# First gates and values moved into the front, the last step reordered, and decay rows carried by 9 transfers per sequence in place of 24

## The reference

```python
alpha = jax.nn.sigmoid((x @ Wg + bg) / GATE_NORM)          # one gate per token and head
def step(state, inp):
    qt, kt, vt, at = inp
    state = at[..., None, None] * state + kt[..., None] * vt[:, :, None, :]
    out_t = jnp.einsum('bhk,bhkv->bhv', qt, state)
    return (state, out_t)
...
return out * og @ Wo

gates = jax.nn.softmax(x @ Rw, axis=-1)                     # 3 experts, per token
base = x @ W + b
zg = (x @ A) * gates                                        # LoRA, rank 8 per expert
return base + SCALING * (zg @ Bm)
```

## Time and profile before

| | us |
|---|---|
| median of three runs | 528.37 |
| lowest and highest | 527.98 and 529.04 |
| profiled execution, its own time | 528.53 |
| its span, first to last instruction | 526.4 |
| TensorE busy in the span | 490.9 (93%) |
| VectorE and ScalarE busy | 352.1 (67%) and 341.9 (65%) |
| granted TensorE clock, mean | 0.966 |

### The profile page before, as it was taken

How to read it: one execution, slowest core, us unless ns; L and a number is a source line. 1 busy time by engine, 2 the same in 40 slices (tenths; PEclk the granted TensorE clock), 3 DMA queues, 4 the chain that set the end, 5 groups by cost and what they waited for, 6 DMA issues and landing times.

```text
span 526.4 us, 11885 instructions
## 1 busy us (share of the span) xinstructions
PE 490.9 (93%) x4560; PEld 392.3 (75%) x4560; DVE 352.1 (67%) x1012; ACT 341.9 (65%) x647; POOL 170.0 (32%) x241
## 2 busy tenths in 40 slices
PE   8689989998999999998899999999999887999995
PEld 6557867786778778876578787787777676888884
DVE  6887887787777977462587677775778562544533
ACT  3968967795768688955467676676666534565541
POOL 3510550035003102200435727447274441443311
PEclk8879999999999999998899999999999997999998
DMA  8600000000001200000342241231312000001001
GB/s 304 186 1 2 2 0 1 0 2 1 0 1 42 98 1 1 2 0 27 94 116 73 60 112 46 77 90 52 100 46 76 2 3 0 22 21 40 21 21 41
DMA packets 24251, 23.44 MB, mean 45 GB/s; under 512 B 3809, under 2 KB 22945, under 8 KB 24065
## 3 DMA queue, kind: packets, MB, share of 16 engines
q1 hardware_dynamic: 23136, 22.12, 13.8%
q10 hardware_dynamic: 1056, 0.52, 0.4%
HBM read 20.27 MB, written 2.36 MB: 43 GB/s over the span
## 4 chain that ended last, share of the span: by engine, by line
PE 43%; ACT 4%; DVE 2%; issue 2%; POOL 2%; DMA 1%; SPq 1%; DVEq 0%; POOLq 0%; ACTq 0%
PE bank L2044 6%; PE bank L1958 5%; PE bank L168 5%; PE bank L170 5%; PE bank L169 5%; PE bank L1983 3%; PE bank L2009 3%; PE bank L1998 3%; PE bank L1971 2%; PE bank L2036 2%; PE bank L244 2%; ACT att_qT L1773 1%; PE bank L2052 1%; ACT lora_zT L1769 1%; DVE att_prob L1420 1%
## 5 line engine op out<-in xcount | busy, mean ns | idle before, releaser
L1069 PE MATMUL bank<-ffn_g_hi,w_hi 128*128 128x512 f32 x288 | 116.8, 406 | 0.1
L1070 PE MATMUL bank<-ffn_g_lo,w_hi 128*128 128x512 f32 x288 | 114.1, 396 | 0.0
L610 DVE TENSOR_TENSOR ffn_g_lo<-ffn_full,ffn_g_hi 128x512 fp32r<-128x512 f32 x96 | 67.1, 699 | 27.4 <-ACT ffn_full L856 26.0
L1069 PEld LDWEIGHTS bank<-ffn_g_hi,w_hi 128*128 128x128 f32 x288 | 54.3, 189 | 13.9 <-issue 1.7
L1070 PEld LDWEIGHTS bank<-ffn_g_lo,w_hi 128*128 128x128 f32 x288 | 54.3, 189 | 11.7
L856 ACT ACTIVATE ffn_full<-bank,cols 128x512 f32<-128x512 f32 x64 | 44.3, 697 | 20.9 <-PE bank L1070 14.7
L1608 POOL TENSOR_TENSOR att_vw<-att_v,att_prob 128x128 f32<-128x128 f32 x64 | 25.2, 421 | 88.1 <-DVE att_prob L1420 88.1
L1800 ACT COPY att_qT<-bank 128x512 f32<-128x512 f32 x64 | 37.1, 589 | 12.8 <-PE bank L170 8.6
L1420 DVE TENSOR_TENSOR_SCAN att_prob<-att_prob,bank 128x512 f32<-128x512 f32 x32 | 37.4, 1204 | 7.7 <-DMA att_prob<-cut_rows 7.6
L1431 DVE TENSOR_TENSOR att_prob<-bank,att_prob 128x512 f32<-128x512 f32 x32 | 21.9, 691 | 29.8 <-PE bank L1958 27.8
L712 POOL TENSOR_TENSOR ssm_out_rstd<-ssm_out_var,neg_half 128x4 f32<-128x4 f32 x8 | 9.2, 1154 | 82.3 <-DVE ssm_out_var L491 82.3
(11 more groups left out here) (230 smaller groups left out, 1181.8 us busy)
## 6 DMA issues: line engine op xcount, KB each, us to landing
att_prob<-cut_rows SPq DMA_DIRECT2D x64, 128.0 KB, 3.0
att_wide<-cum_rows SPq DMA_DIRECT2D x64, 56.0 KB
out<-att_vw SPq DMA_DIRECT2D x7, 256.0 KB, 2.3
x<-in_x SPq DMA_DIRECT2D x3, 512.0 KB, 11.8
w_raw<-in_w_all SPq DMA_DIRECT2D x1, 1152.0 KB
w_raw<-in_w_all SPq DMA_DIRECT2D x1, 768.0 KB, 9.6
x<-in_x ACTq DMA_DIRECT2D x2, 256.0 KB, 3.5
w_raw<-in_w_all SPq DMA_DIRECT2D x1, 512.0 KB, 4.8
```

The costliest lines, as they stand in the source:

```text
L610: dve.tensor_tensor(lo, full[j % 4][:, :], hi.bitcast(F32), ALU.subtract).then_inc(low, 1)
L1069: pe.matmul(acc, w[0], x[0], start=start, stop=False)
L1070: return pe.matmul(acc, w[0], x[1], start=False, stop=stop)
```

## The change

Three things are edited. **One:** the gates and values matmuls of sequence 0 stand in the front, the gates behind tile 21 of the last pair, the values at its very end, and ScalarE's gates and the save of `cut` there too. VectorE then runs all four scans of sequence 0 ahead of its first `weigh`. **Two:** in step 7 the router of sequence 0 and 1, the exponentials, `join`, `low_h`, `down(1)` and `flip_in(9)` have other places. **Three:** the DRAM copies of `cut` and `cum` have another layout, and a sequence takes 9 transfers in place of 24.

```diff
-        r["cut_rows"] = nc.dram_tensor("cut_rows", (B, NH, 2, Q), F32, kind="Internal").ap()
-        r["cum_rows"] = nc.dram_tensor("cum_rows", (B, NH, S), F32, kind="Internal").ap()
+        r["cut_rows"] = nc.dram_tensor("cut_rows", (B, 2, GLO, Q), F32, kind="Internal").ap()
+        r["cum_rows"] = nc.dram_tensor("cum_rows", (B, GLO, S), F32, kind="Internal").ap()
...
+def save_cut(sp, r, b, saved):
+    for u in range(2):
+        rows = r["cut_rows"][b, u].rearrange("g (t n) -> t g n", n=C)
+        sp.dma_start(rows, r["cut"][b % 2][:, u * C:(u + 1) * C]).then_inc(saved, 16)
...
-                    for t in range(T):
-                        sp.dma_start(r["cut_rows"][b, :, :, t * C:(t + 1) * C], by_chunk(cut[b % 2][gate_rows(t), :])).then_inc(cut_saved, 16)
...
-                    for t in range(T):
-                        sp.dma_start(r["cum_rows"][b, :, t * P:(t + 1) * P], cum[b % 2][gate_rows(t), :]).then_inc(cum_saved, 16)
+                    sp.dma_start(r["cum_rows"][b].rearrange("g (t n) -> t g n", n=P), cum[b % 2][:, :]).then_inc(cum_saved, 16)
...
                     for q in range(2):
-                        for u in range(2):
-                            heads = r["cut_rows"][b, g * PER + 2 * q:g * PER + 2 * q + 2, u, :]
-                            sp.dma_start(prob[n % KEEP][half_rows(u), 2 * q:2 * q + 2, :], over(heads, 0, [C, 2, Q])).then_inc(spread_in[n % KEEP][q], 16)
+                        first = g * PER + 2 * q
+                        heads = r["cut_rows"][b, :, first:first + 2, :].rearrange("u h n -> u (h n)")
+                        dst = prob[n % KEEP][:, 2 * q:2 * q + 2, :].rearrange("p h n -> p (h n)")
+                        sp.dma_start(dst, over(heads, 1, [2, C, S])).then_inc(spread_in[n % KEEP][q], 16)
...
-                    for k in range(NH):
-                        rows = slice(k % PER * DV, (k % PER + 1) * DV)
-                        sp.dma_start(wide[b % 2][rows, k // PER, C:S], r["cum_rows"][b, k:k + 1, C:S].broadcast_to([DV, S - C])).then_inc(wide_ready, 16)
+                    for q in range(2):
+                        heads = r["cum_rows"][b, q * PER:(q + 1) * PER, C:S]
+                        dst = wide[b % 2][:, q, C:S]
+                        sp.dma_start(dst, over(heads, 1, [PER, DV, S - C])).then_inc(wide_ready[b % 2], 16)
...
+                                if j == 21:
+                                    gate_mm(pe, claim(pe, "alpha", 0), r, r["h_full"][0]).then_inc(mm, 1)
...
+                    for k in range(2):
+                        value_mm(pe, claim(pe, "ahead", k), r, [x[:, :] for x in h[0]], k).then_inc(r["ahead"], 1)
...
-                alpha(0)
-                values(0)
                 for k in range(AHEAD):
                     query(0, k)
...
-                for j in range(LEAD):
+                for j in range(PAIRS):
                     scan(0, j)
...
+                    if not n:
+                        route(0, 0)
                     weigh(b, 2)
                     weigh(b, 3)
-                    if not n:
-                        route(0, 0)
...
+                across(LAST, 0)
+                route(1, 0)
+                across(LAST, 1)
                 moments(B + 2)
-                route(1, 0)
...
-                    join(b)
+                        join(b)
+                low_h(B + 1)
+                join(LAST)
+                rescale(B + 2)
                 gate(LAST)
-                low_h(B + 1)
-                rescale(B + 2)
```

More of the change, by code:

```diff
@@ L94, in build @@
         r["wg"] = sb("wg", [P, GLO])
+        r["cut"], r["start"] = [sb(f"cut{n}", [P, P]) for n in range(2)], sb("start", [P, P])
+        r["ahead"], r["cut_saved"] = ctx.enter_context(nc.semaphore("ahead")), ctx.enter_context(nc.semaphore("first_cut_saved"))
         r["ones"] = sb("ones", [P, P])
@@ L396, in loop_uses @@
                         uses.append((("spread", j - 9), 6 + j - 15))
+                    if i == 3 and j == 21:
+                        uses.append((("alpha", 0), 6))
                 uses.append((("y", 2 * i), 4))
             uses += [(("y", B - 1), 5), (("yflip", B - 2), 4), (("yflip", B - 1), 5)]
+            uses += [(("ahead", 0), 0), (("ahead", 1), 1)]
             return uses
@@ L763, in _ @@
                     pool.wait_ge(att_h_ready, b + 1)
-                    pool.tensor_tensor(h[b][1][:, :], r["h_full"][b][:, :], h[b][0][:, :].bitcast(F32), ALU.subtract)
+                    pool.tensor_tensor(h[b][1][:, :], r["h_full"][b][:, :], h[b][0][:, :].bitcast(F32), ALU.subtract).then_inc(att_h_low, 1)
+                for tile in (*r["cut"], r["start"]):
+                    pool.memset(tile[:, :], 0.0).then_inc(blank, 1)
             @block.scalar
@@ L955, in _ @@
                     bring_y(2 * i)
+                act.wait_ge(blank, SLOTS + 1)
+                act.wait_ge(bias_kept, 1)
+                act.wait_ge(mm, full_at("alpha", 0))
+                cut_gates(act, r, r["cut"][0], bank("alpha", 0))[0].then_inc(cut_ready, 1)
                 bring_y(B - 1)
@@ L1212, in attention_lora @@
         og = pair("og", [P, 2, S])
-        cut, cum = pair("cut", [P, P]), pair("cum", [P, P])
-        start = sb("att_start", [P, P])
+        cum = pair("cum", [P, P])
         ends, total = pair("ends", [P, NC, NH]), pair("total", [P, NC, NH])
@@ L1335, in __init__ @@
             def __init__(self):
-                self.made = 0
+                self.made = GIVEN
             def __call__(self, pe, *use):
@@ L1549, in _ @@
                     weigh(b, 1)
-                    scan(b, 2)
-                    scan(b, 3)
+                    if b:
+                        scan(b, 2)
+                        scan(b, 3)
                     if n:
@@ L1794, in values @@
                     for k in range(2):
-                        act.wait_ge(ring_mm, full("v", b, k))
+                        if b:
+                            act.wait_ge(ring_mm, full("v", b, k))
+                        else:
+                            act.wait_ge(r["ahead"], k + 1)
                         act.copy(v[s][:, 2 * k:2 * k + 2, :].rearrange("p c n -> p (c n)"), bank("v", b, k)[:, :]).then_inc(v_ready, 1)
@@ L1843, in _ @@
                 keep_htok(0)
-                for b in range(B):
-                    n = b + 1 < B
-                    if n:
-                        gates(b + 1)
+                for b in range(LAST):
+                    gates(b + 1)
                     for k in range(AHEAD, NH):
@@ L1850, in _ @@
                     out_gates(b)
-                    if n:
-                        values(b + 1)
+                    values(b + 1)
                     keep_states(b)
                     keep_inner(b, 0)
-                    if not n:
-                        exps(0, 0)
                     normalise(b + 2)
-                    if n:
-                        for k in range(AHEAD):
-                            query(b + 1, k)
-                    else:
-                        ranks(0, 0)
-                        for m in range(KH):
-                            relu(0, m)
+                    for k in range(AHEAD):
+                        query(b + 1, k)
                     keep_inner(b, 1)
-                    if n:
-                        keep_total(b + 1)
+                    keep_total(b + 1)
                     bring_h(b + 2)
-                    if n:
-                        keep_htok(b + 1)
+                    keep_htok(b + 1)
+                for k in range(AHEAD, NH):
+                    query(LAST, k)
+                out_gates(LAST)
+                act.activation(table[:, :], r["neg_half"][:, :], ACT.Exp)
+                exps(0, 0)
+                keep_states(LAST)
+                keep_inner(LAST, 0)
+                normalise(B + 1)
+                ranks(0, 0)
+                for m in range(KH):
+                    relu(0, m)
+                    if m == 1:
+                        bring_full(B + 1)
+                    if m == 2:
+                        bring_high(B + 1)
+                keep_inner(LAST, 1)
                 exps(1, 0)
+                ranks(1, 0)
                 normalise(B + 2)
-                ranks(1, 0)
                 for b in range(1, B):
@@ L1914, in alpha @@
                     ps = claim(pe, "alpha", b, 0)
[L1915 to L1917 removed]
+                    gate_mm(pe, ps, r, hT[b % 2]).then_inc(ring_mm, 1)
                 def values(b):
@@ L2082, in _ @@
                             query(b + 1, k)
-                    else:
-                        flip_ranks(0, 0)
-                        for m in range(KH):
-                            layer1(0, m)
-                    inside(b, 1)
-                    cross(b, 0)
-                    if n:
+                        inside(b, 1)
+                        cross(b, 0)
                         totals(b + 1)
-                    flip_in(b + 2)
-                    if n:
+                        flip_in(b + 2)
```

(10 more changed lines are left out.)

112 lines of the change are left out of this document (60 added, 52 removed).

## The result

The changed kernel takes 620.29 us, median of 4 executions (619.29 to 621.16), beside 528.17 for the kernel before (526.04 to 529.04): the ratio is 1.175, with an interval of 1.171 to 1.179. It is 92 us slower. The forecast was 613 (592 to 655), with the mechanism of two DMA engines.

What follows compares the result with a forecast made beforehand. Two DMA engines per spread were taken to bound the kernel: sequence 0's data at 265.1, sequence 1's 304.3, six periods of 31.7 to 494.5, `states` 496.7, plus 117.8 - 5.4 + 1.6, plus 2.1 outside: 613 us, range 592 to 655.

Steps and rivals of the forecast that it cites:

- Two engines per spread: Engines divide both sides' outermost sizes; a spread reading [2, C, S] into 128 partitions gets 2. Forecast's chance 0.77.
- The rival of sixteen engines: Chance 0.13: split by SBUF or write side, spreads run on 16 engines, steps stay 21.4 us, end 516.3.
- Time of one spread: 131,072 B on each of two engines at 24.5 GB/s: 5.35 us, within 5.06 and 6.4; four make 21.4.
- The front: Start of sequence 0: front ends about 240.6, block starts 241.9, first spread packets move at 243.3 us.
- The period: Time per sequence in later steps: busiest engine 28.1 us plus 3.6 for turn-rounds, 31.7; six of them.
- turn-rounds: Empty queue between a save's last packets and the next spread's first: 1.8 us, twice per sequence, 3.6.
- First interval, last data to last data: From sequence 0's last scan data to sequence 1's, with both att_wide sets between: 8.2 + 2 x 4.8 + 21.4 = 39.2 us.
- The tail: From sequence 7's `states` to the end: 117.8 us, less 5.4 (2 to 7) for step 7's new order, plus 1.6.
- the lower clock: TensorE enters `states` of sequence 7 after long idling and runs at half clock: 1.6 us lost.
- `normalise` waiting for `join` and `rescale`: In step 7's new order, `normalise`, and `flip_in` with it, wait for these: some 1.9 us lost.
- The rival of instruction loads stuck behind full engines: Chance 0.06: TensorE's code loads wait behind 5.35 us transfers, 20 us per step, half hidden: 683 us.
- It decides from some 5 engines on: Engine count separating the cases: at 4 a sequence takes 21.0 us, even with the step.

Runs made afterwards that it cites:

- all on 16: Changed kernel with each spread cut into two halves and att_wide sent by single heads, so both use 16 engines; saves left: 513.47 us, ratio 0.969.

## Why the forecast came out, step by step

**Two engines per spread: right, and shown.** Cutting the transfers so that 16 engines take part gives back 107 us, and 4 engines in place of 2 give 66 (620.3 to 554.1). The rival of sixteen engines, at 516.3, describes the repaired kernel (513.5). The rule of the Trainium skill that I had cited holds in all of these; its row in the section "Rules for kernel authors" on using all 16 engines (DMA: Bandwidth & Descriptors) even names a short outermost dimension as the trap. Another row of that table would have led into it: it calls two transfers to the two halves of the partitions a waste and asks for one over 128. Here the measurement decides against that row as it stands, because in this layout the one transfer has the two halves outermost.

**Time of one spread: 5.35 forecast, 5.12 measured,** 25.6 GB/s per engine, at the fast bound of the earlier trace rows. The last data of sequence 0 were forecast for 265.1 and came at 264.50.

**The front: 241.9 forecast for the block's start, 240.95 measured.** In the other executions with this front SyncE issues the first spread between 240.93 and 242.47, so the forecast lies inside the scatter. With two engines per spread the front is worth 2.9 us at `states` of sequence 7. Where they don't bind, it brings 4.9 to 7.8 us in three profiles; the rival of sixteen engines had 6.8.

**The period: 31.7 forecast, 32.99 measured.** This is the term that was too small. My 28.1 + 3.6 against the measured parts:

- Spreads, four times 5.12 = 20.5, where I had 21.4. `att_wide` 4.8 forecast, and 4.83 by the run without it.
- What is left is 33.0 - 20.5 - 4.8 = 7.7, and I had 1.9 for the saves and 3.6 for the two turn-rounds, 5.5. So the halves of the loop have 2.2 us more in them than I took from the earlier trace rows, where a save went by an empty queue. The GB/s of the changed kernel between 341.2 and 354 us have a piece in them in which one of two engines seems to be idle:

```profile
GB/s 45 51 51 51 51 51 51 51 51 64 93 82 30 26 38 26 26 26 26 26 51 51 51 51 51 102 51 51 51 51 51 51 51 51 51 51 38 42 22 0
```

The eight slices at 26 to 38 (0.32 us each) are the rate of one engine; they follow the save of `cum`, and a like piece of 2.4 us stands in the other half of the period. At a turn-round the engines move nothing for 1.5 us, as the slices of 0.1 us from 339 to 343 show, and as long around 354 and 373:

```profile
GB/s 33 38 36 36 28 3 0 0 0 0 0 0 0 0 0 0 0 0 0 0 0 20 41 20 41 82 41 41 41 82 41 41 41 82 41 41 41 82 41 41
```

By my estimate from these slices the 7.7 us are 3.0 for two turn-rounds (I had 3.6), 2.5 lost to the two pieces at half rate (I had nothing), and 2.2 for the saves (I had 1.9). So the term that I had left out is the half rate. Why one engine would stop there was not tried, and stays open.

**First interval, last data to last data: 39.2 forecast, 41.6 measured** (264.50 to 306.09). Less 20.5 for the spreads and 9.7 for two sets of `att_wide`, 11.4 are left for three saves and three turn-rounds, and I had 8.2 for them: 1.1 too little for each, as in the period.

**The tail: too small a term, in the other direction.** I had 5.4 for the new order, within 2 and 7, less 1.6 for the lower clock. The changed kernel has 617.3 - 507.23 = 110.1 us from `states` of sequence 7 to the end, where before had 117.8: 7.7, not 3.8. Three things make up the 3.9, to 0.1.

- The low stretch of the clock over `layer1` of sequence 0, 1.7 us, which I hadn't priced, is in the kernel before alone. The new order by itself is worth 6.0 to 6.5: 116.1 with the old one against 110.1 and 109.6 (513.3 - 403.7) with the new one.
- I had charged 1.9 us for `normalise` waiting for `join` and `rescale`. The only gap of TensorE near there in the changed kernel is this, 0.7 less:

```profile
531.88 0.66 PE L246 MATMUL bank<-cols,norm_out 128*128 128x128 f32 x4 [1.20 <-ACT norm_out L1801]
```

- The lower clock, for which I had charged 1.6, came as forecast but cost nothing. In the changed kernel TensorE works through the 8.27 us behind the start of `states` at 0.83 without a gap. In the kernel with the new order alone it has the full clock there and waits 0.78 and 0.76 us for ScalarE; both take 110.1 us to the end.

```profile
507.23:515.50 8.27, 8.27 (x116) 6.51 (x115) 5.04 (x16) 4.12 (x11) 5.00 (x13) 0.83 0.01 2
```

Before, waits of 1.43 and 2.67 stood near the gap of 1.20, and 5 us at a clock of 0.51 behind them. Now the clock keeps its upper level, 2.4 GHz, as I had reckoned:

```profile
526.00:539.00 13.00, 11.37 (x76) 9.60 (x75) 4.74 (x29) 6.51 (x14) 7.69 (x11) 1.00 0.00 0
```

**Sum.** The last scan's data of sequence 7 were 9.55 us later than forecast (504.05 against 494.5): -0.6 for the first sequence, 2.4 for the first interval, 6 x 1.29 for the others. From there to `states` it took 3.2 us in place of 2.2, and the tail gave 3.9 back: 6.6 in the span, 617.3 against 610.7. So the mechanism was right, and that the sum comes as near as 7 us is partly luck: in the period, spreads and turn-rounds priced too high hide part of the term left out, and the tail gave back 3.9 of the 9.55.

**Code loads.** The rival of instruction loads stuck behind full engines (683) did not occur: the steps are even (from sequence 1 on `states` start 32.7 to 33.8 us apart).

**"It decides from some 5 engines on."** With 4 it should have been even with the step; the run with spreads on 4 engines was 36 us slower than with 16. Two things were wrong in that sentence: the halves of the loop, 2.2 us too short, and the mean step, which I took for all steps. Even `att_wide` alone on 4 engines costs 4.6 us, in one step.

## What to carry to other kernels

Before merging transfers, write down the outermost size of both sides; in all runs here the rates and completions agree with as many DMA engines as the largest number up to 16 that divides both. The broadcasts over partitions kept 16 where the repeated dimension (64 or 32) was the outermost one, so two transfers of half the size can be nearly three times as fast as one (141 GB/s against 51 here). Read a DMA share near 1/8 with a flat rate (here 51 GB/s) as two full engines, not as idle ones.

Fewer transfers do save issue time, here 1.1 us for two on SyncE against 3.6 to 5.0 for eight, but that counts only for what is queued behind them. The version with the urgent transfer moved ahead of the eight is 1.8 us faster without merging anything. And a mean step hides the crowded one: check the step in which two sequences' transfers meet by itself.

## What the runs showed of the hardware

- The issue of a DMA itself can block. With 2 engines per transfer the first four spreads took SyncE 10.20 us to issue, where eight on 16 engines took 4.97, and a save behind them 4.99 where it took 0.55 with all on 16. The next item of SyncE was a wait for that save, so no cost of it shows here. First the changed kernel, then all on 16:

```profile
240.91 10.20 SPq L1749 DMA_DIRECT2D att_prob<-cut_rows  x4
251.16 4.99 SPq L1737 DMA_DIRECT2D cum_rows<-att_cum  x1
```
```profile
242.47 4.97 SPq L1750 DMA_DIRECT2D att_prob<-cut_rows  x8
247.49 0.55 SPq L1737 DMA_DIRECT2D cum_rows<-att_cum  x1
```

- One DMA engine moved rows of 2 KB at 25.6 GB/s, evenly: the scans that wait for it are 5.13, 5.12 and 5.12 us apart. With 16 engines the same rows went at 141 GB/s in a share of 0.443, which is 19.9 GB/s for each engine while it is busy (141 / (16 x 0.443)). Eight times the engines brought 2.8 times the rate over this window, which has the start and the end of the transfers in it. The window is 243 to 251 us with all on 16:

```profile
DMA packets 773, 1.13 MB, mean 141 GB/s; under 512 B 132, under 2 KB 260, under 8 KB 772
...
q1 hardware_dynamic: 772, 1.11, 44.3%
```

- `att_wide` on 4 engines (rows of 1,792 B) took 4.83 us for 458,752 B, 23.7 GB/s per engine, where the old form on 16 engines had 13.9.
- Three executions (on three chips) of the same instructions differ by up to 2.9 us at `states` of sequence 7 (400.8, 401.5, 403.7), 1.5 of it already at the first spread's issue (240.95 against 242.47) and 2.1 at sequence 1 (272.7 against 274.8). One profile is too coarse for terms of that size.
